# State space stage of a decoder kernel: part of the products with C moved from VectorE to GpSimd

## What is computed

```python
xr = x @ w_in + b_in
xc, res = jnp.split(xr, 2, axis=-1)
u = jax.nn.silu(_causal_conv(xc, w_conv, b_conv))
x_dbl = u @ w_x
dt, B, C = jnp.split(x_dbl, [DTR, DTR + N], axis=-1)
delta = jax.nn.softplus(dt @ w_dt)
deltaA = jnp.exp(delta[..., None] * A)
deltaBu = delta[..., None] * B[:, :, None, :] * u[..., None]
# h = a * h + bu along the sequence, hs holds every h
y = jnp.einsum('bldn,bln->bld', hs, C) + u * D
return y * jax.nn.silu(res) @ w_out
```

## Time and profile before

| | before |
|---|---|
| median of three executions | 3444.28 us (3443.8 to 3452.95) |
| the profiled execution, own time | 3446.75 us |
| its span in the profile | 3444.8 us |
| mean granted TensorE clock | 0.883 of full speed |
| VectorE scans of the stage, first and last start | 1668.4 and 2215.6 us |
| busy over the span: PE, DVE, ACT, POOL | 80%, 57%, 39%, 41% |

### The profile page before, as it was taken

How to read it: one execution, slowest core, us unless ns; L and a number is a source line. 1 busy time by engine, 2 the same in 40 slices (tenths; PEclk the granted TensorE clock), 3 DMA queues, 4 the chain that set the end, 5 groups by cost and what they waited for, 6 DMA issues and landing times. The chain is left out here.

```text
span 3444.8 us, 72909 instructions
## 1 busy us (share of the span) xinstructions
PE 2755.0 (80%) x28239; PEld 1918.5 (56%) x28239; DVE 1954.5 (57%) x4206; ACT 1330.5 (39%) x2252; POOL 1425.9 (41%) x1537
## 2 busy tenths in 40 slices
PE   4987784998999979786778888695777999993394
PEld 2654453996777755564233333253446888883394
DVE  2654554115767646633599898845565665644123
ACT  3432221441111124321666666352233666651153
POOL 2544443223212145253577777633452111113555
PEclk8988876999999999798899999896788999995697
DMA  6000001660000010033000000000000000001275
GB/s 230 2 1 1 1 1 43 172 175 13 3 3 3 3 46 14 1 115 121 0 1 0 1 1 0 1 1 1 1 2 11 7 7 5 5 2 45 91 230 158
DMA packets 98053, 130.50 MB, mean 38 GB/s; under 512 B 31088, under 2 KB 76528, under 8 KB 97264
## 3 DMA queue, kind: packets, MB, share of 16 engines
q1 hardware_dynamic: 82768, 109.30, 10.5%
q0 software_dynamic: 7168, 14.78, 1.2%
q10 hardware_dynamic: 7776, 1.77, 0.2%
HBM read 103.64 MB, written 25.35 MB: 37 GB/s over the span
## 5 line engine op out<-in xcount | busy, mean ns | idle before, releaser
L661 POOL TENSOR_SCALAR arena<-arena 128x4 f32<-128x4 f32 x120 | 27.5, 229 | 1044.4 <-DVE arena L653 794.1
L2625 POOL TENSOR_TENSOR arena<-arena 128x512 f32<-128x512 f32 x256 | 319.1, 1270 | 141.9 <-ACT arena L2556 141.2
L2686 DVE TENSOR_TENSOR_SCAN arena<-ps,arena 128x512 f32<-128x512 f32 x256 | 312.1, 1219 | 41.3 <-ACT ps L2567 22.5
L2438 PE MATMUL ps<-arena,const_w 128*128 128x512 f32 x512 | 279.2, 629 | 12.6 <-DVE arena L2694 11.5
L163 PEld LDWEIGHTS ps<-L_attn_w,arena 128*128 128x128 f32 x1984 | 241.7, 193 | 53.6 <-issue 42.5
L163 PE MATMUL ps<-L_attn_w,arena 128*128 128x128 f32 x1984 | 257.9, 281 | 8.0 <-POOL arena L2638 3.4
L2567 ACT ACTIVATE ps<-arena,aneg 128x504 f32<-128x504 f32 x256 | 174.4, 681 | 120.0 <-DVE arena L2686 119.8
L1765 PE MATMUL ps<-arena,L_attn_w 128*128 128x512 f32 x384 | 184.5, 617 | 0.9 <-ACT arena L725 0.9
L429 ACT ACTIVATE arena<-ps 128x1024 f32<-128x1024 f32 x96 | 98.3, 1024 | 223.9 <-PE ps L331 223.9
L1833 ACT ACTIVATE arena<-ps,L_attn_w 128x512 f32<-128x512 f32 x64 | 44.0, 687 | 332.6 <-PE ps L1765 332.6
L2694 DVE TENSOR_TENSOR arena<-arena,ps 128x512 f32<-128x512 f32 x256 | 170.0, 665 | 0.0
(11 more groups left out here) (454 smaller groups left out, 6730.7 us busy)
## 6 DMA issues: line engine op xcount, KB each, us to landing
arena<-zone_w SPq DMA_DIRECT2D x54, 512.0 KB
arena<-pair_w SPq DMA_DIRECT2D x40, 578.0 KB
arena<-rt SPq DMA_DIRECT2D x24, 384.0 KB
pair_in<-pair_free SPq DMA_DIRECT2D x1, 5200.0 KB, 28.8
arena<-pair_in SPq DMA_DIRECT2D x40, 130.0 KB
arena<-ctx SPq DMA_DIRECT2D x16, 256.0 KB, 2.9
arena<-pair_out SPq DMA_DIRECT2D x16, 256.0 KB, 5.0
arena<-arena SPq DMA_DIRECT2D x108, 32.0 KB, 2.2
```

The lines of the kernel that those rows point to most:

```text
L2438: pe.matmul(acc(c), e.ident, hc(m, c), start=(k == 0), stop=(k == N - 1)).then_inc(s["acc_mm"], 1)
L2625: q.tensor_tensor(bu(m, c), du(g, c), bs(m), ALU.mult).then_inc(s["bu_done"], 1)
L2686: v.tensor_tensor_scan(hs(m, c), at(c), bu(m, c), 0.0, ALU.mult, ALU.add).then_inc(s["hs_done"], 1)
```

## The change

In every odd state (k = 1, 3, ..., 15) the product with C for the second half of the channels (c = 1) is taken by GpSimd and no longer by VectorE. GpSimd can't read the row of C where TensorE left it, so ScalarE copies that row to SBUF first (`copy_c`, into a new pair of buffers `cs`). VectorE keeps the other three of four products. The orders change with it: GpSimd does `inputs(m+1)` and then `product(m-1)`; ScalarE does `copy_c(m+1)` between `copy_b(m+2)` and `decay(m+1, 1)`; TensorE adds GpSimd's product one step later than before, as the first thing of its step. The waits of all of them follow.

```diff
+    by_pool = lambda m, c: c == 1 and m % 2 == 1
+    products = lambda m: 3 * (m // 2) + 2 + (m % 2)
...
-        bs = room.pair(GT)
+        bs, cs_b = room.pair(GT), room.pair(GT)
+        cs = lambda m: cs_b(m // 2)
...
             def accumulate(m, c):
...
-                    pe.wait_ge(s["hc_done"], 2 * m + c + 1)
+                    if by_pool(m, c):
+                        pe.wait_ge(s["hp_done"], m // 2 + 1)
+                    else:
+                        pe.wait_ge(s["hc_done"], products(m) - (c == 0 and m % 2 == 0))
...
             for m in range(M):
                 g, k = m // N, m % N
+                if by_pool(m - 2, 1):
+                    accumulate(m - 2, 1)
                 accumulate(m - 1, 0)
                 b_row(m + 2)
                 c_row(m + 1)
-                accumulate(m - 1, 1)
+                if not by_pool(m - 1, 1):
+                    accumulate(m - 1, 1)
...
+            def copy_c(m):
+                if m < M and by_pool(m, 1):
+                    a.wait_ge(s["c_mm"], m + 1)
+                    if m >= 4:
+                        a.wait_ge(s["hp_done"], m // 2 - 1)
+                    a.activation(cs(m), cbank(m), ACT.Copy).then_inc(s["cs_done"], 1)
...
                 decay(m + 1, 0)
                 copy_b(m + 2)
+                copy_c(m + 1)
                 decay(m + 1, 1)
...
+            def product(m):
+                if m >= 0 and by_pool(m, 1):
+                    q.wait_ge(s["hs_done"], 2 * m + 2)
+                    q.wait_ge(s["cs_done"], m // 2 + 1)
+                    if m >= 2:
+                        q.wait_ge(s["acc_mm"], summed[m - 2, 1])
+                    q.tensor_tensor(hc(m, 1), hs(m, 1), cs(m), ALU.mult).then_inc(s["hp_done"], 1)
...
                 inputs(m + 1)
+                product(m - 1)
...
             def scan(m, c):
...
-                if m >= 2:
-                    v.wait_ge(s["hc_done"], 2 * (m - 2) + c + 1)
+                if m >= 2 and by_pool(m - 2, c):
+                    v.wait_ge(s["hp_done"], (m - 2) // 2 + 1)
+                elif m >= 2:
+                    v.wait_ge(s["hc_done"], products(m - 2) - (c == 0 and m % 2 == 0))
...
             def contribute(m, c):
-                if m >= 0:
+                if m >= 0 and not by_pool(m, c):
```

More of the change, by code:

```diff
@@ L2342, in state_space @@
     M = NG * N
+    by_pool = lambda m, c: c == 1 and m % 2 == 1
+    products = lambda m: 3 * (m // 2) + 2 + (m % 2)
+    summed = {}
+    for m in range(M + 2):
+        for state, c in ((m - 2, 1), (m - 1, 0), (m - 1, 1)):
+            if 0 <= state < M and (by_pool(state, c) if state == m - 2 else not by_pool(state, c)):
+                summed[state, c] = len(summed) + 1
     use = ssm_order()
     names = PN_SEMS + ("zeroed misc_mm misc_cp taps_done u_done res_done hi_done parts_own bc_parts relu_done sp_own sp_done "
-                       "dl_done du_done b_mm c_mm b_cp a_done bu_done hs_done hc_done acc_mm yo_done yr_done")
+                       "dl_done du_done b_mm c_mm b_cp a_done bu_done hs_done hc_done acc_mm yo_done yr_done cs_done hp_done")
     with block_of(nc, "state_space", names) as (block, s):
@@ L2428, in c_row @@
                     if m >= 2:
-                        pe.wait_ge(s["hc_done"], 2 * m - 2)
+                        pe.wait_ge(s["hc_done"], products(m - 2))
                     row_of(cbank(m), m // N, N + m % N).then_inc(s["c_mm"], 1)
             def accumulate(m, c):
-                if m >= 0:
+                if 0 <= m < M:
                     g, k = m // N, m % N
@@ L2670, in _ @@
                     ln.rstd(q, g + 2)
+            product(M - 1)
             gated(NG - 1)
@@ L2683, in scan @@
                 v.wait_ge(s["bu_done"], 2 * m + c + 1)
-                if m >= 2:
-                    v.wait_ge(s["hc_done"], 2 * (m - 2) + c + 1)
+                if m >= 2 and by_pool(m - 2, c):
+                    v.wait_ge(s["hp_done"], (m - 2) // 2 + 1)
+                elif m >= 2:
+                    v.wait_ge(s["hc_done"], products(m - 2) - (c == 0 and m % 2 == 0))
                 v.tensor_tensor_scan(hs(m, c), at(c), bu(m, c), 0.0, ALU.mult, ALU.add).then_inc(s["hs_done"], 1)
             def contribute(m, c):
-                if m >= 0:
+                if m >= 0 and not by_pool(m, c):
                     v.wait_ge(s["hs_done"], 2 * m + c + 1)
                     v.wait_ge(s["c_mm"], m + 1)
+                    if m % 2:
+                        v.wait_ge(s["cs_done"], m // 2 + 1)
                     if m >= 2:
-                        v.wait_ge(s["acc_mm"], 2 * (m - 2) + c + 1)
+                        v.wait_ge(s["acc_mm"], summed[m - 2, c])
                     v.tensor_tensor(hc(m, c), hs(m, c), cbank(m), ALU.mult).then_inc(s["hc_done"], 1)
@@ L2697, in skipped @@
                 for c in range(2):
-                    v.wait_ge(s["acc_mm"], 2 * N * g + 2 * N - 1 + c)
+                    v.wait_ge(s["acc_mm"], summed[N * g + N - 1, c])
                     v.scalar_tensor_tensor(out=u(g, c), in0=u(g, c), scalar=W("D")[:, c:c + 1], in1=acc(c),
```

## The result

The change makes the kernel slower: 3471.56 us, the median of four executions (3465.29 to 3477.59), against 3445.35 (3443.8 to 3452.95). The ratio is 1.0065, with an interval of 1.0050 to 1.0079. A second set of runs on another chip, beside that chip's own runs of before, gave 1.0066 (1.0053 to 1.0079). By the ratio that is 22.4 us, by these two medians 26.2; 20.7 were forecast, and the measured median stands 6.6 us above the forecast time of 3465.0.

What follows compares the result with a forecast made beforehand. VectorE sets the pace on average, but GpSimd has no room around state 11. +0.7 - 0.6 + 3.8 - 0.8 = +3.1 us in seven periods, less 1, gives +20.7: 3465.0 us; forecast 3456 to 3474, stated range 3447 to 3480.

Steps and rivals of the forecast that it cites:

- stretch 1: From `skipped` to the residual: VectorE's saved products are lost in its wait for TensorE, residual later by 0.7 us.
- stretches 2 and 3: Residual to scan of state 8, one product saved, -0.6 us; then to the norm's scaling, +3.8 us (+1.8 at full clock).
- The stop at the skip term: Second half of `skipped` waits for the group's last sum, now behind the first convolution: new stop of about 1.7 us.
- GpSimd's chain to state 11: State 7's product goes ahead of state 11's `inputs`, so the scan of state 11 comes at 2069.5, before at 2068.27.
- The loop over TensorE's wait: GpSimd's product, two `accumulate`s, B's row, ScalarE's copy, decay: scan of state 12, half 1, +1.8 us at 2.4 GHz.
- its term for the clock: In stretch 3, two `accumulate`s and a row at 1.2 GHz after TensorE's stop take 2.0 us more.
- The stop of "nearly 4 us": TensorE idle before GpSimd's product is there, after its matmul ends near 2068.1: nearly 4 us, taken to lower the clock.
- Stretch 4: From the norm's scaling to the next `skipped`: two products saved, 1.2 us, partly given back; bounds -1.2 and 0, -0.8 taken.
- The rival "much slower": Low clock holds through states 12 to 15 and 0 to 3: 2 us more in seven periods, 3479 us; chance 0.1.
- The last group: Only the states on GpSimd, loop rules: about 6.65 us for two states against 6.85, -1 us over five pairs.
- ScalarE's copies: Eight copies of C's row in a period, 0.58 us each, behind the copy of B: costed at nothing; uncovered, 4 us.
- the scans beside a busier GpSimd: Rival that VectorE's scans, 1209 to 1231 ns before, get longer beside a busier GpSimd: given no chance of its own.

Runs made afterwards that it cites:

- order_alone: Kernel before, with only TensorE's order of the change (half 1 sum of odd states one step later), VectorE making all products: ratio 1.0013.
- sum_behind_rows: Changed kernel, but TensorE adds GpSimd's product behind B's row of the same step instead of ahead of it, state 15 excepted: ratio 1.0018.
- clock_kept: Changed kernel with 14 more matmuls, read by nobody, in TensorE's wait in state 11 of the first seven groups: ratio 1.0040.
- copy_alone: Kernel before, with only ScalarE's eight copies of C's row in a group added, read by nobody: ratio 0.9999.
- load_alone: Kernel before, with eight GpSimd products a group into a spare tile, unread, the scan two states on waiting for them: ratio 1.0044.

## Why the prediction was right, point by point

The stretches of the period shown, by the starts of the same instructions in both traces:

| stretch | forecast | measured |
|---|---|---|
| `skipped` to residual | +0.7 us | 18.99 against 17.93: +1.1 |
| residual to the scan of state 8 | -0.6 | 13.53 against 14.18: -0.65 |
| scan of state 8 to the scaling | +3.8 | 22.03 against 18.60: +3.4 |
| scaling to the next `skipped` | -0.8 | 19.68 against 19.87: -0.2 |
| period | +3.1 | 74.23 against 70.58: +3.65 |

One period is a small sample. There are five in each trace that have the norm's scaling and lie between two `skipped`. In the profiled execution of the changed kernel they are 3.3 us longer than before in the mean (2.3 to 4.4), in that of its second set of runs 2.9 (2.4 to 3.5). By stretches the means are +1.1 and +1.0 to the residual, +2.8 and +2.7 from there to the scaling, and -0.6 and -0.8 to the next `skipped`, against +0.7, +3.2 and -0.8 forecast. So the sum came closer than two of its terms: stretch 1 was taken too low and stretches 2 and 3 together too high, and the two errors cancelled.

- *Stretch 1.* The stop at the skip term was forecast at 1.7 us and was 1.84 us here. The residual's wait for TensorE stayed (2.81 against 2.83 us), so VectorE's savings were indeed lost in it. `order_alone` shows the stop with no added load on GpSimd.
- *Stretch 3.* GpSimd's chain to state 11 was right to 0.1 us. The loop over TensorE's wait and its term for the clock were right in kind: `sum_behind_rows` takes the stop at state 12 away, `clock_kept` takes 1.7 of its 2.1 us. The stop of "nearly 4 us" was 3.96.
- *The clock.* The open question of the sum, whether such a stop suffices for the lower clock, was answered with yes: in all ten periods of the two traces of the changed kernel the two sums behind a stop of 3.95 or 3.96 us took 3.15 to 3.78 us. The Trainium skill, TensorE: Matmul & The Clock Gate, Part 1, has two levels of this clock, 1.2 and 2.4 GHz. These traces agree: the granted clock is 0.50 or 1.00, with a sum in 1.91 us or 1.02, and a value between is the mean of a window in which it changed.
- *Stretch 4 was mis-sized in the period of the table:* -0.8 was taken, -0.2 came. The reasoning was off in both directions. The scaling gave nothing back: it stayed at 6.27 us, its four instructions taking 0.34, 1.29, 2.38 and 2.50 us where before they took 0.34, 2.37, 2.49 and 1.30. GpSimd's product of state 11 took the place of an `inputs` in that row. The forecast had no term for what did take it back, the stop of 0.82 us before the second half of state 15. The granted clock was 0.50 from 2024.0 to 2030.8 us, in the sums and rows ahead of this stop. In the ten periods of the two traces the stop (0.50 to 0.82 us) is there in the seven in which this second stretch at the lower clock lasted 6.8 us, and missing in the three in which it lasted 3.4 us; in these three, stretch 4 took 18.7 to 18.8 us, 1.1 us less than the 19.87 before. So the stop goes with the lower clock. The rival "much slower" had the lower clock hold through states 12 to 15 for 2 us a period. It came back in states 14 and 15, as before the change, and cost at most 0.8 us there. No run takes this stop alone away.
- *The last two groups.* Group 6 has no group after next, so it has no norm and no scaling, and the forecast gave it the same +3.1 as the others. It came out at +5.7 us in one trace and +3.9 in the other. In the first VectorE stops seven times behind state 8, for 10.7 us together, where before it stopped three times, for 3.1. That the others can't catch up there, without the 6.3 us of scaling, is argued only. The last group was forecast to save 1 us. It saved 0.85 us in one trace and lost 0.8 in the other, so that term isn't shown. From the first scan to the last `skipped`, which takes in all eight groups, the two traces are 24.3 and 22.4 us longer than before; 20.7 was forecast for the whole.
- *Costed at nothing, and nothing:* ScalarE's copies (`copy_alone`), and the scans beside a busier GpSimd: they took 1189 to 1225 ns, where before they took 1209 to 1231.

## What to carry to other kernels

The average idle time of an engine is no room for new work: 20 us of 71 were free on GpSimd, and two of the eight products fell where it had none, while four others, put where it does wait, made the kernel 0.5% faster. When work moves to another engine, look for whoever waits for it in order, and for what is queued behind that wait; here a row needed two states later stood behind a sum that nobody needed soon, and moving that sum behind it gave back about three quarters of the loss. A group's last item is a special one: it is waited for at once, where the others have two steps of time.

## What the runs showed of the hardware

- Behind each stop of TensorE of 3.95 or 3.96 us, in ten periods of ten, the granted clock fell to 0.50, and two sums took 3.15 to 3.78 us. Behind shorter stops it was at either level: in the changed kernel two sums took 1.98 us behind most stops of 2.1 us, but 3.62 us behind one of them; a stop of 2.62 us at the same place of group 6 was followed by 3.78 us in one trace and 1.98 in the other; and in `clock_kept` a stop of 2.12 us was followed by 2.92 to 3.48 us in five periods of five. So a short stop gives no safety, and one profile doesn't show at which level a stretch will run.
- Filling the stop with 14 matmuls of 0.23 us each kept the clock at 1.00 up to the next stop and made the kernel 9 us faster though it did more.
- VectorE's four scaling instructions took 6.26 to 6.29 us before and after the change, 6.88 us in all five periods of `load_alone`, and 6.60 or 7.22 us in `order_alone`, where GpSimd has no added load. Before and after, the first takes 0.34 us, and each of the other three ends within 0.1 us of the end of an instruction of GpSimd. So what counts is which instructions of GpSimd stand beside them and not how busy it is on average. That wasn't tried by itself.
